# Moving four groups of instructions in a fused state-space and mixture-of-experts kernel

## What is computed

```python
# part 1: a selective state-space layer, gated by a layernorm of x
xp    = in_proj_w @ ctx                       # 256 channels, 256 steps
u     = silu(causal_conv4(xp) + conv_b)
dt_lo, Bm, Cm = split(x_proj_w @ u)           # 8, 16, 16 rows
delta = softplus(dt_proj_w @ dt_lo + dt_proj_b)
state = state * exp(delta * A) + (delta * u) * Bm      # 16 states a channel, step by step
y     = (sum_n state * Cm + D * u) * silu(layernorm(x))
x     = x + y
# part 2: top-2 of 8 experts, at most 320 rows each
xn    = layernorm(x)
probs = softmax(xn @ Wg); take the best two of 8
h     = relu(rows_of_expert @ w1[e])          # 256 -> 1024
eo    = h @ w2[e]                             # 1024 -> 256
x     = x + gate * eo, added back to each row's token
```

## Time and profile before

| what | us |
|---|---|
| median of three runs | 296.43 |
| lowest, highest | 295.77, 297.27 |
| the profiled execution, its time | 295.34 |
| the profiled execution, its span | 293.5 |
| PE, DVE, POOL, ACT busy in the span | 243.5, 225.5, 213.8, 173.4 |
| one expert, first low piece to first low piece | 16.2 |

### The profile page before, as it was taken

How to read it: one execution, slowest core, us unless ns; L and a number is a source line. 1 busy time by engine, 2 the same in 40 slices (tenths; PEclk the granted TensorE clock), 3 DMA queues, 4 the chain that set the end, 5 groups by cost and what they waited for, 6 DMA issues and landing times.

```text
span 293.5 us, 5022 instructions
## 1 busy us (share of the span) xinstructions
PE 243.5 (83%) x1564; PEld 219.7 (75%) x1564; DVE 225.5 (77%) x372; ACT 173.4 (59%) x379; POOL 213.8 (73%) x174
## 2 busy tenths in 40 slices
PE   8967693958687696896799999989999999999950
PEld 7745573647555575795789998979989898989940
DVE  3799998999999999999887569294857768494510
ACT  2799669658996774576356373654727363645200
POOL 1689599969979999998538368576676858586562
PEclk9999889799869755589999999999999999999995
DMA  7589610080006441141226752636455462635110
GB/s 165 220 247 320 228 73 0 11 315 1 0 3 212 148 142 38 38 179 39 72 81 218 222 184 71 255 131 222 177 206 176 150 230 72 241 118 178 37 53 28
DMA packets 15073, 40.38 MB, mean 138 GB/s; under 512 B 2922, under 2 KB 9900, under 8 KB 12112
## 3 DMA queue, kind: packets, MB, share of 16 engines
q1 hardware_dynamic: 11792, 33.15, 33.3%
q0 software_dynamic: 2816, 6.32, 6.3%
q10 hardware_dynamic: 448, 0.70, 0.9%
HBM read 32.72 MB, written 8.49 MB: 140 GB/s over the span
## 4 chain that ended last, share of the span: by engine, by line
POOL 21%; issue 15%; DMA 13%; PE 11%; DVE 8%; ACT 6%; POOLq 1%; DVEq 0%; ACTq 0%; SPq 0%
DMA w2raw<-in_w 10%; POOL out L491 6%; POOL w2lo L472 5%; POOL dbu L358 5%; ACT hthi L747 3%; ACT w2hi L642 3%; DVE h L1283 2%; POOL expert_rows L403 2%; DVE eo L1496 2%; DVE hc L1302 2%; PE ps L1063 2%; PE ps L1065 2%; PE ps L1064 2%; PE ps L868 1%; DMA xe<-expert_rows 1%
## 5 line engine op out<-in xcount | busy, mean ns | idle before, releaser
L358 POOL TENSOR_TENSOR dbu<-du,bsb 128x1024 f32<-128x1024 f32 x31 | 72.7, 2365 | 1.2 <-DMA bsb<-b_rows 0.9
L581 ACT ACTIVATE ps<-delta,anegs 128x255 f32<-128x255 f32 x128 | 53.1, 462 | 13.4 <-DVE h L1283 9.6
L1485 DVE SCALAR_TENSOR_TENSOR htlo<-ps,hthi 128x320 fp32r<-128x320 f32 x64 | 30.3, 486 | 34.8 <-ACT hthi L747 34.7
L846 PE MATMUL ps<-stack,sels 64*128 64x256 f32 x64 | 17.8, 366 | 31.8 <-DVE hc L1302 28.9
L868 PE MATMUL ps<-cst,hc 128*128 128x128 f32 x256 | 42.5, 320 | 1.4 <-DVE hc L1302 1.4
L472 POOL TENSOR_TENSOR w2lo<-w2raw,w2hi 128x512 fp32r<-128x512 f32 x28 | 35.6, 1297 | 10.9 <-ACT w2hi L642 10.7
L846 PEld LDWEIGHTS ps<-stack,sels 64*128 64x128 f32 x64 | 11.3, 222 | 40.2 <-issue 39.8
L1283 DVE TENSOR_TENSOR_SCAN h<-ps,dbu 128x1024 f32<-128x1024 f32 x18 | 41.1, 2281 | 0.2
L1063 PE MATMUL ps<-xthi,w1hi 128*128 (+1 forms) x124 | 39.2, 316 | 0.3 <-ACT w1hi L635 0.3
L1063 PE MATMUL ps<-hthi,w2hi 128*128 128x320 f32 x112 | 35.8, 320 | 3.6 <-POOL w2lo L472 3.6
L491 POOL DMA_INDIRECT out<-eo,dst x24 | 24.5, 1022 | 19.1 <-DVE eo L1496 13.6
(11 more groups left out here) (185 smaller groups left out, 512.7 us busy)
## 6 DMA issues: line engine op xcount, KB each, us to landing
w1raw<-in_w SPq DMA_DIRECT2D x8, 1024.0 KB
w2raw<-in_w SPq DMA_DIRECT2D x8, 1024.0 KB, 4.8
bsb<-b_rows SPq DMA_DIRECT2D x7, 1024.0 KB, 7.3
expert_rows<-fill SPq DMA_DIRECT2D x1, 2580.0 KB, 15.8
xe<-expert_rows SPq DMA_DIRECT2D x8, 258.0 KB, 5.3
out<-x SPq DMA_DIRECT2D x4, 256.0 KB, 5.2
xnat<-in_x SPq DMA_DIRECT2D x1, 768.0 KB, 7.3
xe<-expert_rows SPq DMA_DIRECT2D x8, 64.5 KB, 5.7
```

The costliest lines, as they stand in the source:

```text
L358: nc.gpsimd.tensor_tensor(dbu[j % DRING][:], du[:, :, None, cols(b)].to_broadcast([P, EC, 2, L]), bsb[b % 2][:, None, 2 * p:2 * p + 2, :]. ...
L581: ins = nc.scalar.activation(decays(g % SLOTS_DA)[:, c, i * L + 1:(i + 1) * L], delta[:, c, b * L + 1:(b + 1) * L], ACT.Exp, scale=anegs[: ...
```

## The change

Four edits:

- `gated_rows(e-1)` stands on DVE behind the third `htlo` of expert e (f = 2), no more behind the fifth.
- POOL makes all its low pieces of `w2` of an expert (four; two in the last expert) before it sends the results of the expert before.
- The statistics of z are taken in two steps of three tiles (p = 1 and 2), with the variance behind p = 2, no more in three steps of two with the variance behind p = 3.
- `z_rstd(2, ...)` stands on POOL between `softplus_d(1)` and `softplus_w(1)`, no more between `softplus_delta(1)` and `delta_u(1)`.

```diff
@@ POOL, loop over the steps
                     if p == 3:
                         softplus_d(b + 1)
+                        if b == 0:
+                            z_rstd(2, slice(BT, TILES))
                         softplus_w(b + 1)
                     if p == 4:
                         softplus_delta(b + 1)
-                        if b == 0:
-                            z_rstd(2, slice(BT, TILES))
                         delta_u(b + 1)
@@ POOL, experts
-                for m in range(0 if e else WP // 2, WP // 2 if e == NE - 1 else WP):
+                pieces = range(0 if e else WP // 2, WP // 2 if e == NE - 1 else WP)
+                for m in pieces:
                     low_w2(e, m)
-                    if m == WP // 2 - 1 and e >= 1:
+                    if m == pieces[-1] and e >= 1:
                         send_results(e - 1)
                 fetch(e)
@@ DVE, loop over the steps
-                    if p in (1, 2, 3):
-                        ins = z_stats(range(2 * p, 2 * p + 2))
-                    if p == 3:
+                    if p in (1, 2):
+                        ins = z_stats(range(3 * p - 1, 3 * p + 2))
+                    if p == 2:
                         z_variance(range(BT, TILES), ins)
@@ DVE, expert
-                    if f == 4 and not first:
+                    if f == 2 and not first:
                         gated_rows(e - 1)
```

## The result

The changed kernel takes 300.37 us (median of four runs, 299.76 to 302.91), the kernel before beside it 296.48 (295.77 to 297.27). The ratio is 1.0108 (95% interval 1.0059 to 1.0156): 1.1% slower, where 1.6% faster was forecast.

The account below looks back on a forecast made before the run. DVE was taken to bound the scan stage, GpSimd's ring with PE's gap the experts, GpSimd the end. Savings of 1.0 (scan) and 3.8 (GpSimd's path) make 4.8 us, from 296.43 to 291.6; range 286.5 to 296.0.

Parts of the forecast that it names:

- PE's gap behind `w2lo`: Expert stage: PE waits for a low piece of w2, costing about 0.9 us an expert; removing it saves 5.4 us of PE time.
- the ring that makes it: Expert stage: GpSimd waits 1.91 us for gated rows, sends, makes the last low pieces; then SyncE loads w2, ending GpSimd's next wait.
- if so_far has landed: Expert stage, DVE: condition on the gated rows starting 1.7 us earlier, behind the third htlo.
- The landing: GpSimd's loop: third send lands 6.3 us behind the w2 load's issue, between 5.9 and 7.2, giving a 16.3 us loop.
- the hand-over terms: GpSimd's loop besides the landing: low pieces and step 5.2, landing to first fetch 0.9, fetches and next low piece 3.9 us.
- the second rival: Expert stage: third send lands 7.6 us behind the load, loop 17.6, kernel slower at 299.4 us; chance 0.12.
- The sum over the path: GpSimd, expert 1's first low piece to last expert's first send: 103.2 us falls to 99.4, 3.8 less.
- The scan stage: Product for sequence 1's first scan comes 2.2 us earlier, ending DVE's 1.10 gap: 1.0 us saved, range 0 to 1.2.
- the third rival: Scan stage gives nothing, because the later scans make PE late: 292.6 us; chance 0.11.
- The first, sends that land as quickly as before: Expert stage: sends land in 2.0 us, GpSimd's loop is 14.7, PE paces experts at 15.3: 287.1 us; chance 0.17.
- the row of the scatters: Trace evidence against quick sends: a scatter behind a 1 MB load took 4.4 us, against 2.0 to 2.5 without one.
- The sign set down for "wrong": Expert stage: sends still 2.4 and experts 15.3 us, or a new DVE wait for so_far lengthening an expert beyond 16.5.

Follow-up runs that it names:

- the case 290.4: Kernel before with only the gated rows moved to f = 2, low pieces two and two around the sends as before: 290.44 us, ratio 0.9809.
- both cures: Changed kernel with the next expert's rows read later and the w1 load issued behind the sixth hidden chunk: 290.98 us, ratio 0.9775.
- the kernel with the rows apart: Changed kernel with the next expert's rows read about 5 us later, so only the w2 load is beside the sends: 291.95 us, ratio 0.9763.

## Why the prediction was wrong

**What bounds the kernel: half right.** PE's gap behind `w2lo` and the ring that makes it were seen, and that an expert without PE's gap takes 15.3 to 15.4 (all rounds of the gated rows alone). What was not seen is that the gated rows alone close the gap: they free GpSimd's 1.91 us of idle time ahead of the sends, and all low pieces follow from it. The prediction costed the two expert edits as one sum, and so never met the case 290.4.

**Gated rows: the mechanism right, the cover overrated.** They start behind the third `htlo`, and in quiet rounds cost nobody anything. "PE's last hidden chunk needs the fourth, and has 0.8 us of slack left" was the warning; the step that failed is the condition "if so_far has landed", which got no price. It fails in two of six loop experts, by 3.3 and 3.5 us; its other waits are below 0.8.

**The landing: the term that was mis-sized.** 6.3 us behind the load was taken; 7.15 to 7.45 was measured where rows stand behind it. The fetches of before, 7.0 and 7.6, were the right rows to read. The deduction of 0.4 for a write and of 0.3 for an earlier start had no row that showed them. In experts 1 to 6 of the changed kernel a third fetch that is not caught takes 1.98 to 2.04, no longer than the 2.0 of a third send before. And a third send 2.7 us behind the load's issue (7.15 to 7.45) and a third fetch 4.5 us behind it (7.0, in the kernel with the gated rows alone) are there at nearly the same time. With 7.25 the loop is 5.2 + 7.25 + 0.9 + 3.9 = 17.25 by the prediction's own sum, against 16.8 to 17.0 measured, because the hand-over terms were a little too large (the idle time of 3.88 ends 0.9 behind the landing, but low pieces and the fetches took 16.80 - 7.15 - 0.9 = 8.75, not 9.1). So rounds of 16.9 instead of 16.3 are the first part of the miss: about 0.6 in each of four, 2.4 us. The 1.1 for the rows was right (6.15 and 5.85 without them, and 6.1 with the rows moved away).

**The caught fetch: the step that was missing.** The prediction let PE and GpSimd meet no delay from a fetch; two rounds took 18.94 and 17.95 instead of 16.3 and 15.2, and the last expert's two low pieces and the wait for its first send, which there stands 0.96 for rows that follow a late PE, took 3.51 instead of 2.7: 2.6 + 2.8 + 0.8 = 6.2 us. PE's clock, 0.50 behind each of the two waits, is in these 6.2; the prediction had no term for it. The prediction names the catch in one clause of the second rival, "a fetch caught by the next w1 load, with htlo now behind it in DVE's queue and PE behind that", and gives it neither price nor chance, though the loop of 16.3 and PE's round, which issues the w1 load, might have told where the fetch stands: with the fetches after the landing, the third started within 0.3 us of the load in the two long rounds. Neither edit alone has this harm: with the gated rows alone the third fetch lands in 2.0 to 2.8, and with the low pieces alone it is caught, but what stands behind it costs PE 2.0 to 2.2 us and GpSimd nothing.

**The sum over the path.** Forecast 99.4; 2.4 for the landing and 6.2 for the caught fetches make 108.0; measured 107.97. The two amounts are read from this same profile, so the sum is an account and not a test; the test is that without catches (w1 load later) the kernel takes 295.75, and with both harms taken away 290.2 (the w2 load behind the landings) or 291.0 (both cures).

**The scan stage.** 1.0 was taken. The prediction's "only long" gap of DVE before 140 us is not the only one, there is one of 3.52 at 4.78, but that plays no part here. DVE's wait is gone in all eight profiles with the edits, and their first scan of sequence 1 starts at 46.67 to 48.37, where the six without have 47.41 to 49.18; in the times nothing is left of it. This was the third rival, and its reason, PE late, is where the wait at 74 us stands, though that comes without the edits too.

**The rivals.** The first, sends that land as quickly as before, fell: sends took 3.1 to 6.1 us behind the load, not 2.0 to 2.5. With the load moved away GpSimd's idle time was again the 1.96 of a quiet landing and PE paced the loop, at 15.6, as that rival says. So the row of the scatters was the right one to go by. The Trainium skill's "DMA: Bandwidth & Descriptors", section "Queues, rings and completion order", has each DMA engine take a packet of each queue in turn. It gives no time for a small transfer beside a large one; what the prediction drew from it, that a send would hardly notice the load, does not hold here (third sends 3.1 to 4.7 against 2.0). The second rival, 299.4 from a landing of 7.6, is the nearest number (300.37), and it had 0.12. That it is so near is in part luck: it priced a landing of 7.6 in every round, and the catch, which it only named, made up what was missing. That the time fell outside the range comes from pricing the landing below the rows that were closest to it, and the catch not at all.

**Signs.** Right: no gap ahead of sequence 1, no waits for `w2lo`, 3.1 to 4.5 us idle between third send and first fetch, third sends of 3.1 to 4.7 us. Not seen: PE's wait of about 1 us in each expert (it was two waits, 3.4 and 3.8), and the last expert's first send only 0.1 to 0.3 behind its second low piece (it was 0.96). The sign set down for "wrong", a wait of DVE for so_far that lengthens an expert beyond 16.5, is what came.

**The better version.** Gated rows at f = 2 alone, with three low pieces first, or the changed kernel with the w2 load behind the landings: 289.89 to 290.44, not to be told apart, 2% below before. The smallest edit is the one line.

## What to carry to other kernels

When work is moved that releases a large load, list which small transfers are then issued beside it, and price each by the nearest transfer that already runs behind such a load, without deductions. Where a queue of one engine has a landing in its ring, keep work under the landing. A row of work that waits for a small transfer and stands ahead of what another engine needs is only as good as that transfer is punctual: the gated rows gained 6 us where their fetch was never late, and cost PE 6.4 us at once where it was. Look at the granted clock behind each such wait of PE, for the wait alone can be half of the loss. Cost and measure the parts of a joint change one by one: here one line gained 6 us, and the other part, beside it, took 8 to 11 back.

## What the runs showed that was not expected

- A gather that is issued 0.3 us (205.32) or 0.06 us (258.18) *before* a 1 MB load takes 5.2 and 5.4 us instead of 2.0. With the low pieces alone, 0.40 and 0.33 us ahead, it took 5.2 and 5.3. In the kernel with the rows apart, 0.86 us ahead of the load, it took 3.3, and cost its waiter 0.9.
- Third sends land 7.15 to 7.45 us behind the issue of the w2 load with 0.32 MB of rows behind it, and 5.85 to 6.15 without, though they start 2.7 us behind the load. A fetch that starts 4.5 us behind one (gated rows alone, load 196.20, fetch 200.68 and 2.5) is there after 7.0.
- After the same 2.90 us of idle time PE was granted 1.00 in one profile and 0.50 in another.
- Each of the five waits of PE for a caught fetch's `htlo` (3.4 to 3.8 us, in three profiles) was followed by 3.4 or 6.8 us at 0.50. Behind a wait of 2.0 us the clock stayed at 1.00, behind one of 2.2 it fell.
